# Sixteen one-hots per batch move from VectorE to GpSimd, with a ring of six one-tile units

## The reference

```python
x = x + gnn(adj, layernorm(x))     # x: 8 batches of 1024 rows of 128, fp32
x = x + ffn(layernorm(x), route_id)

# gnn: for each row n the first 25 columns (lowest index) with adj[n] != 0
vals, idx = top_k(where(adj != 0, -arange(1024), -inf), 25)
feats = where(valid, X[idx], -inf)
agg = feats.max(axis=2)            # plus max(agg, 0) where the degree is at most 25
out = relu(concat([X, agg]) @ W + b)

# ffn: h = relu(x @ Wi.T + bi); two layers, each
h = relu(h @ Ws[l].T + bs[l] + h @ Wr[l, e].T + br[l, e] + h)   # e: expert of the 128 rows
out = h @ Wo.T + bo
```

## Time and profile before

| | us |
|---|---|
| runs, median of 3 | 750.15 (747.49 to 750.78) |
| the profiled execution | 748.9 |
| its span | 747.2 |
| PE busy | 610.9 (82%) |
| DVE busy | 615.6 (82%), of it L926 106.7 |
| ACT busy | 567.8 (76%) |
| POOL busy | 238.2 (32%), of it L508 202.4 |
| mean granted clock of TensorE | 0.932 |

### The profile page before, as it was taken

One profiled execution on the slowest core, in us unless ns is written; L12 is line 12 of the kernel. 1 busy time (PEld: TensorE's weight loads), 2 busy tenths in 40 slices (PEclk: granted clock), 3 DMA queues, 4 the chain that ended last, 5 costly groups with the idle time before them and its releaser, 6 DMA issues.

```text
span 747.2 us, 11820 instructions
## 1 busy us (share of the span) xinstructions
PE 610.9 (82%) x3496; PEld 501.5 (67%) x3497; DVE 615.6 (82%) x1047; ACT 567.8 (76%) x1053; POOL 238.2 (32%) x260
## 2 busy tenths in 40 slices
PE   0464766769997899969996999788996999799786
PEld 0053644557886688847985788667875888589665
DVE  3775898889998899879998999889987998778740
ACT  5664554679897988889897889797988997678262
POOL 4522225433543324333243413332434234410000
PEclk9997898989999799979997999889997999799989
DMA  9999995399647855695549755874566463135222
GB/s 303 308 191 287 303 349 187 124 236 299 183 134 197 227 146 140 148 254 170 158 110 224 224 142 146 197 226 126 142 156 161 122 165 93 29 84 155 57 70 77
DMA packets 145171, 131.73 MB, mean 176 GB/s; under 512 B 72219, under 2 KB 112324, under 8 KB 145092
## 3 DMA queue, kind: packets, MB, share of 16 engines
q1 hardware_dynamic: 128124, 105.94, 53.0%
q0 software_dynamic: 7296, 15.74, 8.2%
q10 hardware_dynamic: 9680, 9.21, 4.3%
HBM read 98.20 MB, written 17.98 MB: 155 GB/s over the span
## 4 chain that ended last, share of the span: by engine, by line
PE 51%; DVE 26%; issue 8%; ACT 5%; DMA 5%; DVEq 2%; SPq 2%; ACTq 0%
PE slot_ps L730 24%; PE ffn_ps L795 10%; DVE acc L939 9%; DVE onehot L926 5%; PE ffn_ps L805 4%; DMA at<-mask 3%; DVE score L1000 3%; DVE top L998 2%; PE prep_ps L822 2%; DMA adj_sb<-in_adj_dram 2%; PE ffn_ps L745 2%; SPq L393 2%; PE ffn_ps L779 2%; PE ffn_ps L764 2%; DVE wst L1104 1%
## 5 line engine op out<-in xcount | busy, mean ns | idle before, releaser
L730 PE MATMUL slot_ps<-onehot,xsplit 128*128 128x512 f32 (+3 forms) x1376 | 371.2, 399 | 61.8 <-ACT onehot L642 32.9
L939 DVE TENSOR_TENSOR acc<-slot_ps,acc 128x896 f32<-128x896 f32 (+2 forms) x336 | 292.6, 882 | 52.2 <-PE slot_ps L730 45.9
L730 PEld LDWEIGHTS slot_ps<-onehot,xsplit 128*128 128x128 f32 x1376 | 251.0, 204 | 118.3 <-issue 52.4
L508 POOL DMA_INDIRECT gath<-feature_table,idx x200 | 202.4, 1012 | 400.2 <-DMA gath<-feature_table,idx 294.8
L642 ACT ACTIVATE onehot<-away 128x896 fp32r<-128x896 bf16 (+3 forms) x168 | 118.6, 706 | 23.7 <-PE slot_ps L730 10.0
L795 PE MATMUL ffn_ps<-hT,wst 128*128 128x128 f32 x1024 | 135.2, 277 | 0.0
L625 ACT ACTIVATE away<-rank,ranks 128x896 bf16<-128x896 bf16 (+3 forms) x168 | 132.9, 791 | 0.6 <-DVE wst L1104 0.6
L795 PEld LDWEIGHTS ffn_ps<-hT,wst 128*128 128x128 f32 x1024 | 129.0, 191 | 5.7 <-issue 0.6
L926 DVE TENSOR_SCALAR onehot<-rank,ranks 128x896 fp32r<-128x896 bf16 (+3 forms) x128 | 106.7, 834 | 0.0
L584 ACT ACTIVATE hT<-ffn_ps,wst 128x128 f32<-128x128 f32 x256 | 81.1, 374 | 33.4 <-PE ffn_ps L795 31.7
L596 ACT ACTIVATE rank<-prep_ps 128x448 bf16<-128x448 f32 x128 | 62.9, 549 | 24.4 <-PE prep_ps L822 12.9
(11 more groups left out here) (120 smaller groups left out, 528.8 us busy)
## 6 DMA issues: line engine op xcount, KB each, us to landing
wst<-folded_weights SPq DMA_DIRECT2D x128, 257.0 KB
adj_sb<-in_adj_dram SPq DMA_DIRECT2D x64, 512.0 KB
folded_weights<-wst ACTq DMA_DIRECT2D x34, 256.0 KB
hT<-in_L_ffn_Wr_dram SPq DMA_DIRECT2D x26, 256.0 KB
xs<-in_x_dram SPq DMA_DIRECT2D x8, 512.0 KB
feature_table<-xn SPq DMA_DIRECT2D x8, 512.0 KB
x<-in_x_dram SPq DMA_DIRECT2D x8, 512.0 KB
out_dram<-h SPq DMA_DIRECT2D x16, 256.0 KB, 2.7
```

The lines of the kernel that those rows point to most:

```text
L508: pool.indirect_dma_start(gath[:, j, :], None, tables[b], bass.IndirectOffsetOnAxis(ap=idx[:, b % 2, h, j:j + 1], axis=0)).then_inc(signal ...
L730: mm = pe.matmul(slot_ps[n % 2][:, c0:c1], xsplit[:, b % 2, part, first + j, :], onehot[:, n % RING, j, c0:c1], start=(j == 0 and part == ...
L939: dve.tensor_tensor(acc[:, p % 2, 0:cols], slot_ps[n % 2][:, 0:cols], acc[:, p % 2, 0:cols], ALU.max).then_inc(s_max, 1)
```

## The change

GpSimd makes the 16 one-hots that VectorE made (POOL_HOT; L547 of the new kernel), by the same instruction; VectorE makes none (DVE_HOT is empty), ScalarE keeps its 28. GpSimd now walks through the positions too: one-hots five positions ahead, the split at position 20, and each gather at a position of its own, in two tables (at 29 to 42 of a stage and 0 to 24 of the next; for the first batch at 0 to 26), without waits between the gathers. ScalarE's one-hots go from three to five positions ahead. The ring has six units of one tile: a slot takes one unit or two, and a function works out which, and which earlier slot must be done (FREE).

```diff
-AHEAD = 3
-RING = 3
+ACT_AHEAD = 5
+POOL_AHEAD = 5
+DVE_AHEAD = 4
+UNITS = 6
-PACE = 2
+POOL_HOT = [3, 5, 7, 13, 15, 16, 18, 19, 20, 23, 24, 31, 33, 36, 38, 42]
+DVE_HOT = [p for p in range(NS) if p not in ACT_HOT and p not in POOL_HOT]
+    SPLIT_AT = 20
+    GATHER_AT = {29: [0], 30: [1], 32: [2], 33: [3], 35: [4], 36: [5], 38: [6], 39: [7], 41: [8], 42: [9]}
...
-        onehot = sb("onehot", [P, RING, 2, COLS], F32R)
+        onehot = sb("onehot", [P, UNITS, COLS], F32R)
...
+        def ring():
+            unit, free, last = [], [], [0] * UNITS
+            u = 0
+            for n in range(B * NS):
+                many = GROUPS[SLOTS[n % NS][0]][1]
+                if u + many > UNITS:
+                    u = 0
+                unit.append(u)
+                free.append(max(last[u:u + many]))
+                for i in range(u, u + many):
+                    last[i] = n + 1
+                u = (u + many) % UNITS
+            return unit, free
...
+            def gather(b, j):
+                part, signal, reduced = (0, s_gathA, s_redA) if j < HALF else (1, s_gathB, s_redB)
+                if j == 0:
+                    pool.wait_ge(s_idx, b + 1)
+                    pool.wait_ge(s_tab[b % 2], 16 * (b // 2 + 1))
+                if j == HALF * part and b > 0:
+                    pool.wait_ge(reduced, b)
+                pool.indirect_dma_start(gath[:, j, :], None, tables[b], ...
+            def one_hot(n):
...
+                if p == min(q for q in POOL_HOT if SLOTS[q][0] == g):
+                    pool.wait_ge(s_q, 2 * IT * b + 2 * (first + many))
+                if FREE[n] > 0:
+                    pool.wait_ge(s_slot, FREE[n])
+                pool.tensor_scalar(onehot[:, UNIT[n]:UNIT[n] + many, 0:wide * P],
+                                   rank[:, b % 2, first:first + many, 0:wide * P], ranks[:, r - 1:r], None,
+                                   ALU.is_equal).then_inc(s_poolhot, 1)
...
-            for b in range(B):
-                for h in range(HUBS):
-                    gather(b, h, range(HALF), s_gathA, s_redA)
-                    gather(b, h, range(HALF, TOPK), s_gathB, s_redB)
-                if b + 1 < B:
-                    split(b + 1)
+            for s, p in positions():
+                n = (s - 1) * NS + p + POOL_AHEAD
+                if 0 <= n < B * NS and n % NS in POOL_HOT:
+                    one_hot(n)
+                if 0 < s < B and p == SPLIT_AT:
+                    split(s)
...
+                        for j in where.get(p, []):
+                            gather(b, j)
...
-                if n >= RING:
-                    act.wait_ge(s_slot, n - RING + 1)
+                if FREE[n] > 0:
+                    act.wait_ge(s_slot, FREE[n])
```

More of the change, by code:

```diff
@@ L56 @@
 SQUARED = [p for p in ACT_HOT if SLOTS[p][1] > 1]
-DVE_HOT = [p for p in range(NS) if p not in ACT_HOT]
+POOL_HOT = [3, 5, 7, 13, 15, 16, 18, 19, 20, 23, 24, 31, 33, 36, 38, 42]
+DVE_HOT = [p for p in range(NS) if p not in ACT_HOT and p not in POOL_HOT]
 AWAYS = 2
@@ L251, in gnn_ffn_program @@
         s_acthot = sem("s_acthot")
+        s_poolhot = sem("s_poolhot")
         s_slot = sem("s_slot")
@@ L314, in positions @@
                     yield s, p
+        def ring():
[11 more added lines that the diff above has]
+            return unit, free
+        UNIT, FREE = ring()
         def norms(s):
@@ L497, in split @@
                                    ALU.subtract).then_inc(s_split, 1)
[L499 to L510 removed]
+            def gather(b, j):
[5 more added lines that the diff above has]
+                    pool.wait_ge(reduced, b)
+                pool.indirect_dma_start(gath[:, j, :], None, tables[b],
+                                        bass.IndirectOffsetOnAxis(ap=idx[:, b % 2, 0, j:j + 1], axis=0)
+                                        ).then_inc(signal, 16)
+            def one_hot(n):
+                b, p = divmod(n, NS)
+                g, r, wide = SLOTS[p]
+                first, many = GROUPS[g]
+                if p == min(q for q in POOL_HOT if SLOTS[q][0] == g):
[5 more added lines that the diff above has]
+                                   ALU.is_equal).then_inc(s_poolhot, 1)
             split(0)
@@ L670, in _ @@
                                    ).then_inc(s_mask, 1)
-                for ahead, body, slots in ((AHEAD, one_hot, ACT_HOT), (AHEAD + 1, distance, SQUARED)):
+                for ahead, body, slots in ((ACT_AHEAD, one_hot, ACT_HOT), (ACT_AHEAD + 1, distance, SQUARED)):
                     n = (s - 1) * NS + p + ahead
@@ L721, in slot @@
                     pe.wait_ge(s_acthot, b * len(ACT_HOT) + ACT_HOT.index(p) + 1)
+                elif p in POOL_HOT:
+                    pe.wait_ge(s_poolhot, b * len(POOL_HOT) + POOL_HOT.index(p) + 1)
                 else:
@@ L730, in slot @@
                             mm = pe.matmul(slot_ps[n % 2][:, c0:c1], xsplit[:, b % 2, part, first + j, :],
-                                           onehot[:, n % RING, j, c0:c1], start=(j == 0 and part == 0),
+                                           onehot[:, UNIT[n] + j, c0:c1], start=(j == 0 and part == 0),
                                            stop=(j == many - 1 and part == PARTS - 1))
@@ L1153, in _ @@
                     fold_slot(s - 1, p)
-                ahead = (s - 1) * NS + p + AHEAD
+                ahead = (s - 1) * NS + p + DVE_AHEAD
                 if 0 <= ahead < B * NS and ahead % NS in DVE_HOT:
```

28 lines of the change are left out of this document (14 added, 14 removed).

## The result

The changed kernel takes 763.02 us (median of four runs, 762.64 to 764.83) where the kernel before takes 748.82: a ratio of 1.0197, with a 95% interval of 1.0157 to 1.0237. It is slower by 14 us; forecast were 723, and 748 as the upper end. The execution with the profile took 764.83 us with a span of 763.1.

What follows compares the result with a forecast made beforehand. In a middle batch no engine is full; TensorE waits in turn for ScalarE's one-hots and VectorE, mostly at slots 9 to 12. 13.9 + 9 + 5 − 2 = 25.9 us off 748.9 gives 723; range 703 to 748.

Steps and rivals of the forecast that it cites:

- What POOL takes over: POOL's 16 one-hots cost 16.5 us per batch at 0.95 us for 896 columns; POOL has 50 us of work, none late.
- the upper price: POOL's one-hots priced like a two-input tensor_tensor, 2.16 ns an element: 37 us per batch, costing back 7 to 14 us.
- Rival 3: POOL is the bound: a one-hot costs three times the lower price, 83.4 us of work per batch, 769 us; chance 0.10.
- the dense place: Positions 8 to 20: eight one-hots, eight gathers and the split, 21 us of POOL work against 23 us, none late.
- Rival 4: Nothing moves: upper price and several collisions per batch eat the gain, 748 us; chance 0.08.
- term D: New collisions of POOL's SBUF reads with DVE's two-input instructions: 2 us taken, 14 us at one per batch in seven batches.
- part A: Slots 10 and 12: one-hots two positions earlier win 2.2 us per middle batch; 13.9 us in all, bounds 0 and 32.
- B: DVE without its 16 one-hots, 13.9 us of its time per batch: 9 us off PE's waits, bounds 0 and 11.9.
- Relieving it of these does nothing here: At the halt before slots 10 to 12, taking one-hots off DVE wins nothing: none of its work since 395.12 was one-hots.
- C: First batch, 42.7 to 147.1 us: DVE is the bound, its one-hots' time counts; 5 us, between 0 and 7.9.
- Rival 1: The halt gets so short that the granted clock stays up: 705 us; chance 0.20.
- Gathers at positions: POOL's waits for its own earlier gathers go, those for the list of rows are hidden by the lead; counted at 0.

Runs made afterwards that it cites:

- Experiment 12: A kernel of its own timing POOL instruction forms at three widths and DVE beside them; at 896 columns a cast takes 0.93 us, a tensor_scalar 2.45 to 2.53.
- experiment 6: The changed kernel with slot 13's one-hot made by DVE, the fifteen others by POOL; 749.24 us, ratio 0.9959.
- experiment 3: The changed kernel with POOL writing only 64 columns of each of its one-hots, all waits and gathers kept; 725.67 us, ratio 0.9651.
- experiment 2: The kernel before with the six-unit ring, ACT five ahead and DVE four; DVE makes the 16 one-hots, gathers in blocks, two in flight; 744.72 us, ratio 0.9916.
- experiment 8: The changed kernel with ten one-hots on POOL, six on DVE (slots 13, 15, 16, 19, 23, 42), each gather waiting for its position's slot; 729.58 us.
- experiment 4: The changed kernel with POOL's one-hots half as wide (448 of 896 columns); 728.89 us, ratio 0.9705.
- 1: The changed kernel with the 16 one-hots back on DVE, gathers at their positions without waits between them; 873.76 us, ratio 1.1648.
- 7: The changed kernel with the 16 one-hots back on DVE and each gather waiting for the slot before its position; 749.51 us, ratio 0.9975.
- experiment 11: As experiment 6, but POOL writes zeros to an unused buffer (three memsets of 1.6 us) where slot 13's one-hot was; 760.4 us, ratio 1.0146.
- 9: The kernel of experiment 8 without the gathers' waits for their slots; 730.35 us, ratio 0.974.

## Why the prediction was wrong

**The step that failed is "What POOL takes over".** It priced a one-hot of 896 columns at 0.95 us and bounded it by 2.12; it takes 2.545. Both ends were from rows, but neither row was of this operation: of the lower price, 182 ns at one column is an affine select and 292 ns at 128 a cast, and the `tensor_tensor` was held to be the dearer form only because it has more inputs. "I take the lower, since it has one input too" took the number of inputs for what sets the price. Experiment 12 shows that it does not: a cast and a `tensor_scalar` have one input each and take 0.93 and 2.53 us. Per batch the one-hots take 44.6 us, not 16.5 or 37.

The Trainium skill, "GPSIMD Engine Reference", section 3.1, gives 1.03 cycles per element for bodies of up to two operations and 2.6 for a two-input `tensor_tensor`. The runs agree with the order of cast and `tensor_tensor` (0.93 and 2.07 us) and not for the form at issue: one operation, one tensor, 2.45 to 2.53 us. Its agreement with my lower price was no second witness.

**What that price did to the path.** Two things.

First, lateness. The prediction had at the upper price "some slots come 1 to 2 us late"; at the true one PE waits 1.3 us for POOL in each middle batch and 3.44 in the eighth. Rival 3 had the right mechanism with a chance of 0.10, and put its point of decision at 46.1 us of one-hots per batch, for POOL to be full. POOL was at 44.6 and not full: it still waited 25.5 us in six batches for PE's slots, since a one-hot cannot begin before its unit is free. A maker that can't run far ahead is late at the dense place before its total reaches the batch's length. The prediction's own sum for that place shows it, with the measured prices: 23.6 us of one-hots, 10 of gathers and 2.4 of the split are 36 us against 23, of which the lead of five positions, 9 us, covers a part. That 763 lies close to this rival's 769 is luck: its condition was not met, and some 14 us of the 763 go with the one-hot of slot 13 alone (experiment 6). Rival 4, with 0.08, is nearer in kind: a dear one-hot and several collisions together. It only let them stop at 748.

Second, collisions, term D. I had 2 us for the whole kernel and 14 at most, because "DVE is idle more than before" and one was to cost up to 2.1 us (in the kernel before, a one-hot of 1024 columns beside the split had already taken 3.61 us in another batch, 2.9 more than alone). L1007 alone is 14.6 us longer in six batches (15.8 against 1.2): what blocks it is an instruction of 4.8 us and no longer the split of 2.4. DVE lost 13.9 us of one-hots per batch and is down by 8.8. Of the 5.1 us between, about 4 are in blocked instructions (2.4 in L1007, 1.2 in L1066, 0.3 in L1013); busy time does not fall by the full 13.9 in experiment 3 either, where none is long (11.7). And slack on the average does not cover an instruction that stands in front of the fold which PE waits for. L1007 with 2.4 us per batch stands just there, in the five microseconds that part A had found to be the halt. With that one-hot off POOL a batch is 2.1 us shorter (experiment 6), some 14 us in the time of the kernel.

The Trainium skill, "SBUF — State Buffer", section "Who interferes with whom", says that two-input DVE instructions contend with GpSimd instructions that read SBUF. I had weighed that rule and given it too little; L1007 (195 to 2631 ns), L1066 (545 to 1150) and experiment 12 agree with it. Of DVE's 2-port modes, which `tensor_scalar` can enter by this section, it says that whoever issues first has the shared pair for the whole instruction. For `tensor_scalar` the trace agrees (122.38 of 122.34 in experiment 12); an instruction with two inputs was let in 1.3 us earlier.

**What was right.** *A*, in kind: experiment 2 has the waits where and behind whom they were to be. Its size was too large: 1.3 us per batch at slots 9 to 12 for 2.2, and 7.9 us between the medians for 13.9. That the batch got 2.1 us shorter is luck, for the rest comes from the collision that B had counted. "Relieving it of these does nothing here" was wrong for slot 12, whose wait goes down to about 0.5 us only where DVE has no one-hot of slot 13 to make (the change and experiment 3; 1.4 to 1.5 in 2, 6 and 8). *A, B and C together*: experiment 3, the change with short instructions on POOL, gives 725.67 us for a forecast of 723, and 76.4 us per batch for 76.6. Between the first and the last of the eight sums of `aggT` that close a batch (145.7 and 676.8 us there, 145.9 and 700.0 before) it wins 23.0 us, where A + B − 2 had 20.9, so the sum holds though A and B share it otherwise. *C*, from the first fold to the first `aggT`, was 103.2 us before and is 99.9 there and 98.6 in experiment 4, so 3.3 and 4.6 for 5; both kernels start their slots 2.4 to 3.1 us later, so this is rough. *ACT's one-hots*: the waits for them are gone from the middle batches. *Rival 1*: the clock did not stay up. In the change the halt grew, and at 76.4 us per batch the mean clock was no better than 0.935 over the span (0.932 before). One sum of the prediction does not come out: B and C at their ends give 717 to 737 us as the forecast's own range, not 714 to 732; nothing else rests on it.

**Gathers at positions** were counted at 0. In the change this holds, but by luck: what paced them were the one-hots' waits, of which the prediction says nothing (experiments 1 and 7). Paced by slots they bring nothing (7 against 2).

**How the loss divides, and what stays open.** Experiment 3 at slots 10 and 19, where the change has 4.77 and 1.34 us of idle time:

```profile
392.27 2.54 PE L779 MATMUL slot_ps<-onehot,xsplit 128*128 128x512 f32 x6 [2.68 <-DVE acc L990]
...
408.78 1.96 PE L779 MATMUL slot_ps<-onehot,xsplit 128*128 128x512 f32 x8
```

Over the six middle batches PE's waits before slots are 8.4 us per batch in the change and 4.4 in experiment 3. Of these 4.0 us, 2.4 stand before slot 10, which is the collision with slot 13's one-hot, and 1.3 before slot 19, which is POOL's lateness. The rest of the 4.9 us is mostly PE itself: its busy time is 72.3 us per batch against 71.1, at a mean granted clock of 0.937 against 0.952. How much of that each of the two causes holds is open, and so is whether the collisions elsewhere, of L1066 above all, cost anything; experiment 11, which was to part collision and lateness by time, brought collisions of its own. The 2.1 us more in the first batch are not the one-hots' alone, since experiment 2, with none on POOL, has 1.9 of them. The 1.8 us behind the eighth are probably not the change's: from the last sum of `aggT` to the end it is about 49 us in the change and in experiments 2, 7 and 9, and about 47 in the kernel before and the other eight. What stops all engines during unspaced gathers is not named by the trace.

## What to carry to other kernels

A price for an operation that no row shows must come from its own form: two rows of neighbours are no bounds when the form itself is unknown, and a small kernel that runs it at three widths gives the answer that decides here (2.5 us instead of 0.95). Before moving work to GpSimd, list the VectorE instructions with two SBUF inputs or of `tensor_scalar` that stand in front of what TensorE waits for, and keep GpSimd's long instructions out of those microseconds; ten of the sixteen, chosen by place (experiment 8, 729.58 us), are worth more than all, though no other ten were tried. And when a wait is moved or dropped, ask what else it was spacing.
